# Late rounds of a fused attention and expert kernel: scores in two halves of the features, and a product in three fp32r passes instead of fp32

## The chip, the cores and the metric

One core of a Trainium2 chip. The metric is the device time of one execution in microseconds, the median over runs. Engines: PE (TensorE), DVE (VectorE), ACT (ScalarE), POOL (GpSimd) and SP, which here only issues DMAs.

## What is computed

x is (8, 1024, 256), that is N = 8192 tokens of D = 256. Attention runs over the H = 4 heads of one token, not over the sequence.

```python
xn = _layernorm(x, axis=-1)
q = (xn @ Wq + bq).reshape(b, s, h, d);  k = ...;  v = ...
c, sn = (jnp.cos(phase), jnp.sin(phase))
qr, qi = (q * c, q * sn);  kr, ki = (k * c, k * sn)
scores = (einsum('bshd,bsgd->bshg', qr, kr) + einsum('bshd,bsgd->bshg', qi, ki)) * scale
out = einsum('bshg,bsgd->bshd', softmax(scores, axis=-1), v)
s = swapaxes(out, 1, 2).reshape(b, s, h * d) @ Wo + bo
g = silu(ffn(xn))          # 8 experts, Sinkhorn gates, the best 2 of each token
x = x + s * g
```

## The kernel before

**Stages.** A preparation (layer norm, router, weights split into high and low fp32r parts) is followed by four *early rounds* of attention (q = 0 to 3), the *expert stage* (NM = 135 tiles of up to 128 tokens), and twelve *late rounds* (q = 4 to 15, QE = 4, NQ = 16). A round handles 512 tokens. The change touches the late rounds and adds some work to the expert stage.

**A round** has 24 pieces c on PE, each a 128x512 block of PSUM. Pieces 0 to 15 are q and k (x = c // 8, feature block i = c % 8): six fp32r matmuls each (high by high, high by low, low by high, for two halves of the depth, L1080). ACT writes the cosine part (L817) and DVE, after it, the sine part (L1596) of each piece into QT: a piece is *drained* when both are done. Pieces 16 to 23 are U = xn M, where M is Wv times Wo by heads (L1091): plain fp32 matmuls, two per piece, of XTJ (xn transposed and regrouped by POOL, `xtj`, L577) and M_s. ACT copies each to UN (L824), SP writes it to u_d and reads it back, regrouped, to US. The *scores* (L1027) follow the 24 pieces: four groups n, each 32 fp32 matmuls of 64x64, in two banks in turn.

**Softmax and mix.** DVE reads scores n (`soft_a`: L1484, L1488, L1489, L1490), ACT takes the exponential (L838), DVE normalizes (`soft_b`: L1495 to L1497). In the round after, DVE builds the attention operand (`spread`, L1502 to L1511) and adds the bias to US (`biased`, L1522), PE multiplies (`mix`, L1048) and DVE takes the result out (`mixed`, L1533). Here a `spread` with its `biased` is called a *pair*. Pairs stand at pieces 16, 18, 20 and 22, mixes at 18, 20, 22 and 23, PE's transposes of the next round's tokens (`xt`, L980) at 17 and 20.

**Banks.** Rotated pieces go round five PSUM banks (0, 1, 2, 6, 7), U pieces round three (0, 1, 2). `ring` makes PE wait until the piece that had the bank before is drained.

**The end of a round's tokens.** POOL adds up the two expert outputs and xn of the tokens of round q-1 (`total`, L661 to L668) while PE is in round q, ACT takes their SiLU (`silu`, L804), and POOL finishes them (`result`, L676 and L677). ACT stands in order: `silu(q - 1)` comes behind the copy of piece 18, and ACT then waits for POOL. The first four rounds' tokens are finished by the way in the *host* rounds 5, 7, 9 and 11 (a second `total`, a SiLU between the exponentials, L800), and DVE does their part (`early`, L1544 and L1545) at piece 8 of the round after. For the last round POOL does `total(14)` and `total(15)` in a row, and `silu(15)` stands at piece 23.

**Order.** All of it is written out: each engine runs its own loop over q and c and waits on counters. `s_ch` counts PE's pieces, `s_ca` ACT's, `s_cd` DVE's rotated pieces, `s_xtj` POOL's regroupings, `s_ct` its totals. WR and WM are two views of one stretch of memory of 24576 columns: expert weights in WR, then QT in columns 0 to 16383 and M_s in 16384 to 24575 of WM.

Of the kernel before, what the change touches and what calls it, by code (L numbers as in the profile page):

```python
# [5 lines left out]
F32 = mybir.dt.float32  # L6
# [15 lines left out]
QE = 4  # L22
# [14 lines left out]
def program(nc, x, phase, Wq, bq, Wk, bk, Wv, bv, Wo, bo, rw, rb, temp, wg, wp, wo, out):  # L37
# [8 lines left out]
    with ctx:  # L46
# [7 lines left out]
        m_d = nc.dram_tensor("m_d", [128, 8192], F32).ap()  # L54
        w_d = nc.dram_tensor("w_d", [E * 128, 6144], F32).ap()
# [21 lines left out]
        QT = WM[:, 0:16384].rearrange("p (x c n) -> p x c n", x=4, c=2)  # L77

        def rotated(x, i):

            v = QT[:, x, i % 2, :]
            return v.rearrange("p (t h) -> p t h", h=H)[:, :, i // 2] if x < 2 else v[:, 512 * (i // 2):512 * (i // 2) + 512]
# [3 lines left out]
        XL = sb("XL", [128, 2, 512], F32R)  # L86
        XTJ = sb("XTJ", [128, 2, 4, 128])
        UN = sb("UN", [128, 3, 512])
# [6 lines left out]
        AB = sb("AB", [128, 2, 512])  # L95
        AT = sb("AT", [128, 2, 128])
# [79 lines left out]
        def bank(g):  # L176
            q, c = divmod(g, 24)
            if c < 16:
                return ((0, 1, 2, 4, 5) if q <= QE else (0, 1, 2, 6, 7))[c % 5]
            return (c - 15) % 3  # L180

        held, prior = {}, {}
        for g in range(24 * NQ):
            prior[g] = held.get(bank(g))
            held[bank(g)] = g

        def pM(n):
# [44 lines left out]
            sem(n) for n in ("s_sa2", "s_pm", "s_u63", "s_c15", "s_z", "s_rl"))  # L232

# [56 lines left out]
        def cs(q):  # L290
            if q < NQ - 1:
                return cY1, cY2, cN, cX
            return cE1, cE2, cE3, AB[:, :, :].rearrange("p a (i d) -> p (a i) d", d=D)
# [34 lines left out]
        def _(e):  # L328
# [89 lines left out]
            def load_c(q):  # L418
# [34 lines left out]
            def segment(q0, q1):  # L453
                for q in range(q0, q1):
# [11 lines left out]
                    for c in range(8):  # L466
# [55 lines left out]
            for x in range(1, E):  # L522
# [23 lines left out]
        def _(e):  # L546
# [21 lines left out]
            def xtj(q):  # L568
# [6 lines left out]
                for k in range(2):  # L575
                    for j in range(2):
# [3 lines left out]
                            XL[:, k, :].bitcast(F32).rearrange("p (r j) -> p j r", j=4)[:, 2 * j:2 * j + 2, :], ALU.add)  # L580
                    ins.then_inc(s_xtj, 1)
# [1103 lines left out]
```

## Time and profile before

| | |
|---|---|
| median of 3 runs | 1588.54 us (1585.54 to 1590.78) |
| the profiled execution, its own time | 1590.1 us |
| its span | 1588.3 us |
| PE busy | 1530.9 us (96%) |
| DVE, ACT, POOL busy | 972.8 (61%), 728.8 (46%), 793.0 us (50%) |
| granted TensorE clock, mean | 0.988 |
| share of PE in the chain that ended last | 89% |
| PE L1091 (U), 512 records | 237.1 us |
| PE L1027 (scores), 4096 records | 129.9 us |

Busy time of an engine is the sum over its instructions, and a busy PE can still be a PE that would have had less to do. The chain of work is followed backwards from the last instruction to what released it each time. An fp32 matmul is two records in this profile, an fp32r matmul is one.

### The profile page before, as it was taken

What the parts mean: (1) busy time and instruction counts of PE and PEld (TensorE: products, weight loads), DVE (VectorE), ACT (ScalarE), POOL (GpSimd) and SP (SyncE); (2) the same over time, 40 slices, a digit from 0 to 9 for tenths busy, and PEclk for the clock granted to TensorE, in tenths of its full rate; (3) what the DMA queues carried; (4) which work ended last, traced back from release to release, by engine and by line L of the source; (5) the groups of instructions that cost most, each with busy time, mean ns of one, the idle gap of its engine ahead of it and who ended that gap; (6) DMA issues with size and microseconds to landing.
All of it is one profiled execution on the core that took longest, in us unless ns stands there. A gap on an engine that the chain in (4) does not pass through costs nothing.

```text
span 1588.3 us, 32794 instructions
## 1 busy us (share of the span) xinstructions
PE 1530.9 (96%) x11408; PEld 1166.3 (73%) x11408; DVE 972.8 (61%) x1880; ACT 728.8 (46%) x1205; POOL 793.0 (50%) x945
## 2 busy tenths in 40 slices
PE   5999699989999999999999999999999999999997
PEld 2546566668888888888888888776666776666773
DVE  7567989953333333333333333577889788888777
ACT  4766334413333333333333333546456565555552
POOL 4637589813433444433444333253574564853456
PEclk9999899989999999999999999999999999999999
DMA  9989852265233231323211231255555666455464
GB/s 327 396 314 324 301 187 78 76 217 189 68 124 108 82 126 64 97 95 111 77 54 57 71 146 51 90 167 166 172 187 189 205 200 207 156 168 172 155 206 147
DMA packets 175351, 251.23 MB, mean 158 GB/s; under 512 B 15336, under 2 KB 122656, under 8 KB 175072
## 3 DMA queue, kind: packets, MB, share of 16 engines
q1 hardware_dynamic: 160576, 211.48, 39.1%
q0 software_dynamic: 12960, 35.41, 6.8%
q8 instruction: 104, 1.70, 0.4%
q10 hardware_dynamic: 1664, 2.26, 0.4%
q14 instruction: 47, 0.39, 0.1%
HBM read 149.58 MB, written 99.50 MB: 157 GB/s over the span
## 4 chain that ended last, share of the span: by engine, by line
PE 89%; DVE 6%; DMA 2%; ACT 1%; issue 1%; SPq 1%; ACTq 0%; DVEq 0%
PE ps L1145 23%; PE ps L1080 21%; PE ps L1091 13%; PE ps L1164 12%; PE ps L1027 6%; PE ps L1154 4%; PE ps L1048 2%; PE ps L1127 2%; PE ps L996 2%; PE ps L924 1%; DMA WR<-w_d 1%; PE ps L980 1%; PE ps L914 1%; DVE UN L1230 1%; SPq L502 1%
## 5 line engine op out<-in xcount | busy, mean ns | idle before, releaser
L1145 PE MATMUL ps<-WR,FR 128*128 x1620 | 407.9, 401 | 1.9 <-DMA WR<-w_d 1.8
L1145 PEld LDWEIGHTS ps<-WR,FR 128*128 128x128 f32 x1620 | 296.2, 189 | 60.2 <-issue 3.0
L649 POOL DMA_INDIRECT y_d<-AUX x135 | 133.3, 987 | 351.6 <-ACT AUX L868 351.6
L1656 DVE TENSOR_TENSOR AUX<-AUX,ps 128x512 f32<-128x512 f32 x135 | 92.9, 688 | 342.0 <-ACT AUX L856 342.0
L817 ACT ACTIVATE WM<-ps,bcs,trig 128x512 f32<-128x512 f32 x256 | 252.2, 1016 | 85.9 <-PE ps L1080 78.9
L1596 DVE TENSOR_SCALAR WM<-ps,vec,trig 128x512 f32<-128x512 f32 x256 | 243.6, 993 | 61.2 <-ACT WM L817 60.5
L1091 PE MATMUL ps<-WM,XTJ 128*128 128x512 f32 x512 | 237.1, 600 | 0.0
L856 ACT ACTIVATE AUX<-ps 128x512 f32<-128x512 f32 x135 | 80.9, 599 | 318.5 <-PE ps L1145 318.5
L1080 PE MATMUL ps<-XH,WH 128*128 128x512 f32 x512 | 204.8, 400 | 6.1 <-issue 3.8
L1164 PE MATMUL ps<-WR,ABR 128*128 x1080 | 209.4, 292 | 0.0
L1080 PE MATMUL ps<-XH,WL 128*128 128x512 f32 x512 | 199.7, 390 | 0.0
L1080 PE MATMUL ps<-XL,WH 128*128 128x512 f32 x512 | 199.6, 390 | 0.0
L645 POOL DMA_INDIRECT AUX<-xn_d,AUX x135 | 131.7, 975 | 77.2 <-issue 40.1
L1164 PEld LDWEIGHTS ps<-WR,ABR 128*128 128x128 f32 x1080 | 165.5, 190 | 0.0
L1091 PEld LDWEIGHTS ps<-WM,XTJ 128*128 128x128 f32 x512 | 91.7, 190 | 96.5 <-issue 93.8
L661 POOL TENSOR_TENSOR AUX<-AUX,GP 128x256 f32<-128x256 f32 x128 | 80.3, 662 | 148.3 <-DMA AUX<-in_L_attn_x_dram 144.5
L1164 PE MATMUL ps<-WR,FR 128*128 x540 | 152.1, 282 | 0.0
L1027 PE MATMUL ps<-WM 128*64 128x64 f32 x4096 | 129.9, 227 | 16.8 <-DVE TM L1484 16.0
L1027 PEld LDWEIGHTS ps<-WM 128*64 128x64 f32 x4096 | 126.2, 142 | 25.5 <-DVE TM L1484 16.7
L824 ACT ACTIVATE UN<-ps 128x512 f32<-128x512 f32 x128 | 76.2, 595 | 139.0 <-PE ps L1091 135.9
L1080 PEld LDWEIGHTS ps<-XH,WH 128*128 128x128 f32 x512 | 96.3, 188 | 27.3 <-issue 5.2
L1080 PEld LDWEIGHTS ps<-XH,WL 128*128 128x128 f32 x512 | 96.1, 188 | 20.4
(238 smaller groups left out, 2199.1 us busy)
## 6 DMA issues: line engine op xcount, KB each, us to landing
US<-u_d SPq DMA_DIRECT2D x63, 512.0 KB, 5.4
u_d<-UN SPq DMA_DIRECT2D x120, 256.0 KB, 2.0
WR<-w_d SPq DMA_DIRECT2D x96, 256.0 KB, 6.0
AUX<-y_d SPq DMA_DIRECT2D x32, 512.0 KB, 5.6
WM<-in_L_attn_x_dram SPq DMA_DIRECT2D x16, 512.0 KB, 9.5
xn_d<-WM SPq DMA_DIRECT2D x32, 256.0 KB, 7.3
w_d<-USR SPq DMA_DIRECT2D x16, 512.0 KB, 4.9
AUX<-xn_d SPq DMA_DIRECT2D x16, 512.0 KB, 6.1
```

What stands on the lines that cost most here:

```text
L645: e.indirect_dma_start(XG[:, m % 2, :], None, xn_d, bass.IndirectOffsetOnAxis(gidx[:, m:m + 1], 0)).then_inc(s_g[m % 2], 16)
L649: e.indirect_dma_start(y_d, bass.IndirectOffsetOnAxis(toks[:, m - 5:m - 4], 0), YS[:, (m - 5) % 2, :], None).then_inc(s_y[(m - 5) % 2], 16)
L661: ins = e.tensor_tensor(y[:, i, :], y[:, i, :], GP[:, i, k, q, None].broadcast_to([128, D]), ALU.mult)
L817: e.activation(rotated(2 * x, i), b, ACT.Identity, bias=bcs[:, x, 0, i:i + 1], scale=trig[:, 0, i:i + 1]).then_inc(s_ca, 1)
L856: e.activation(GR[:, :], mG[m % 2][:, :], ACT.Relu).then_inc(s_gr, 1)
L1027: mm = e.matmul(pS[n % 2][row:row + 64, 64 * c:64 * c + 64].rearrange("p (g t) -> p g t", g=H), QT[:, x, h, col:col + 64], QT[:, 2 + x, h, ...
L1080: mm = e.matmul(b[:, :], w[:, k, 128 * c:128 * c + 128], xx[:, k, :], start=(k == 0 and w is WH and xx is XH), stop=(k == 1 and w is WL))
L1091: mm = e.matmul(b[:, :], XTJ[:, k, a // 2, :], M_s[:, k, 512 * a:512 * a + 512], start=(k == 0), stop=(k == 1))
L1145: mm = e.matmul(b[:, :], x, WR[:, bass.ds(off[m] + (2048 * z + 1024 * a + 512 * k), 512)], start=(k == 0 and x is xh and z == 0), stop=(k ...
L1164: mm = e.matmul(mY[m % 2][:, 0:256], x, WR[:, bass.ds(off[m] + (4096 + 1024 * z + 256 * c), 256)], start=(c == 0 and x is hh and z == 0), ...
L1596: e.tensor_scalar(rotated(2 * x + 1, i), ps[bank(24 * q + c)][:, :], bqk[:, x, i:i + 1], trig[:, 1, i:i + 1], ALU.add, ALU.mult).then_inc( ...
L1656: e.tensor_tensor(HS[:, m % 2, :], GR[:, :], mP[m % 2][:, :], ALU.mult).then_inc(s_h, 1)
```

## The change

It applies to the late rounds only.

1. **U in three fp32r passes.** M is kept as a high and a low part (MH, ML). Each U piece is six fp32r matmuls (XHJ by MH, XHJ by ML, XLJ by MH, for two depths) instead of two fp32 ones. POOL's `xtj` (four additions) becomes `xj` (eight copies, of the high and of the low part of xn).
2. **The split of M** is made in the expert stage: sixteen times, once in every seven tiles, ACT issues the load of a 128x512 piece of m_d to UN, DVE splits it (`split_m`, one copy and one subtraction), and ACT issues the store to mhl_d. SP then loads ML and MH (2 x 2 MB and 4 x 1 MB) at the expert stage's end, where it loaded M_s (4 x 1 MB).
3. **Room.** ML takes columns 0 to 8191, MH 16384 to 24575, so that the rotated q and k have 8192 to 16383 (QH), half of what QT had.
4. **Order.** Since QH holds either the even or the odd feature blocks, a late round now runs: the eight even rotated pieces (P0), U 16 to 19, the first half of the scores (`half_scores(q, 0)`, all four groups), the eight odd rotated pieces (P1), U 20 to 23, the second half of the scores. The last round runs P0, U 16 to 23, first half, P1, second half, then its four mixes. Mixes stand at 18, 19, 21, 23, pairs at 16, 17, 19, 20, transposes at 20 and 22; in the last round mixes and pairs keep their places. `soft_a(n)` starts when the second half of the scores of both groups of a bank is there.
5. **Banks.** P0 takes banks 0, 1, 6, 7, 2, 0, 1, 2 in this order (0, 1, 4, 5, 2, 0, 1, 2 in round 4), U 16 to 19 takes 0, 1, 2, 0, P1 takes 1, 2, 6, 7, 0, 1, 2, 0, and U 20 to 23 takes 1, 2, 0, 1.
6. **The x of the last tokens** is loaded late (`load_x`), to the columns of ML that pieces 16 and 17 of the last round have used.

`silu(q - 1)` is still written at piece 18, `early` at piece 8 and `silu(15)` at piece 23; nothing in `total`, `result`, `store_c` or `load_c` of rounds before the last is changed.

```diff
+        def order(q):
+            if q < QE:
+                return tuple(range(24))
+            if q < NQ - 1:
+                return P0 + (16, 17, 18, 19) + P1 + (20, 21, 22, 23)
+            return P0 + tuple(range(16, 24)) + P1
...
+        BANKS = {c: (0, 1, 6, 7, 2, 0, 1, 2)[i] for i, c in enumerate(P0)}
+        BANKS.update({c: (1, 2, 6, 7, 0, 1, 2, 0)[i] for i, c in enumerate(P1)})
...
+            def xj(q):
+                e.wait_ge(s_xtd, 2 * q + 2)
+                e.wait_ge(s_ch, 24 * q)
+                if q == QE:
+                    e.wait_ge(s_dn, NM)
+                for k in range(2):
+                    for v, w in ((XHJ, XH), (XLJ, XL)):
+                        for j in range(2):
+                            ins = e.tensor_copy(v[:, k, 2 * j:2 * j + 2, :],
+                                                w[:, k, :].rearrange("p (r j) -> p j r", j=4)[:, 2 * j:2 * j + 2, :])
                     ins.then_inc(s_xtj, 1)
...
+            def half_scores(q, h):
+                e.wait_ge(s_ca, at(q, 14 + h))
+                e.wait_ge(s_cd, rotated_by[q, 14 + h])
+                if h == 0:
+                    e.wait_ge(s_sm1, 4 * q)
+                for i in range(4):
+                    for c in range(4):
+                        for x in range(2):
+                            for a in range(2):
...
+                                mm = e.matmul(pS[i // 2][row:row + 64, to:to + 64].rearrange("p (g t) -> p g t", g=H),
+                                              QH[:, x, col:col + 64],
...
+                    if h == 1:
+                        mm.then_inc(s_s, 1)
...
                             for k in range(2):
-                                mm = e.matmul(b[:, :], XTJ[:, k, a // 2, :], M_s[:, k, 512 * a:512 * a + 512],
-                                              start=(k == 0), stop=(k == 1))
...
+                                for xx, w in ((XHJ, MH), (XHJ, ML), (XLJ, MH)):
+                                    mm = e.matmul(b[:, :], xx[:, k, j, :], w[:, k, cols],
+                                                  start=(k == 0 and xx is XHJ and w is MH), stop=(k == 1 and xx is XLJ))
...
+                        if q >= QE and c == (23 if q == NQ - 1 else 19):
+                            half_scores(q, 0)
+                    if q >= QE:
+                        half_scores(q, 1)
+                        continue
```

ACT in a late round after round 5, where `silu` stands. Before, it comes behind sixteen rotated pieces and three U pieces:

```order
L817 ACTIVATE WM<-ps7,bcs,trig 128x512
L817 ACTIVATE WM<-ps0,bcs,trig 128x512
L824 ACTIVATE UN<-ps1 128x512
L824 ACTIVATE UN<-ps2 128x512
L753 ACTIVATE XH<-ps3 128x512
L824 ACTIVATE UN<-ps0 128x512
L804 ACT_TABLE_LOAD
L804 ACTIVATE AUX<-AUX 128x1024
L824 ACTIVATE UN<-ps1 128x512
```

The same place in the changed kernel; the rows L903 above the fence are the last of P0, those below `silu` (L890) the first of P1:

```order
L903 ACTIVATE WM<-ps1,bcs,trig 128x512
L903 ACTIVATE WM<-ps2,bcs,trig 128x512
L912 ACTIVATE UN<-ps0 128x512
L912 ACTIVATE UN<-ps1 128x512
L912 ACTIVATE UN<-ps2 128x512
L890 ACT_TABLE_LOAD
L890 ACTIVATE AUX<-AUX 128x1024
L912 ACTIVATE UN<-ps0 128x512
L903 ACTIVATE WM<-ps1,bcs,trig 128x512
L903 ACTIVATE WM<-ps2,bcs,trig 128x512
```

Eight rotated pieces and three U pieces now stand ahead of `silu` in a round, where sixteen and three did; eight rotated pieces stand behind it, where none did.

DVE at the end of the rotated pieces of a late round before (L1596 the last rotation, L1502 to L1522 a pair, L1464 the low part of the next round's tokens, L1533 `mixed`):

```order
L1596 TENSOR_SCALAR WM<-ps0,vec,trig 128x512
L1502 TENSOR_TENSOR AC<-SA,mask8 128x128
L1506 STREAM_TRANSPOSE AC<-AC 128x128
L1507 TENSOR_REDUCE AH<-AC 128x16
L1511 TENSOR_TENSOR AT<-AH,maskr 128x128
L1522 TENSOR_TENSOR US<-US,BR 128x1024
L1464 TENSOR_TENSOR XL<-ps3,XH 128x512
```

and in the changed kernel behind P0:

```order
L1741 TENSOR_SCALAR WM<-ps2,vec,trig 128x512
L1647 TENSOR_TENSOR AC<-SA,mask8 128x128
L1651 STREAM_TRANSPOSE AC<-AC 128x128
L1652 TENSOR_REDUCE AH<-AC 128x16
L1656 TENSOR_TENSOR AT<-AH,maskr 128x128
L1667 TENSOR_TENSOR US<-US,BR 128x1024
L1647 TENSOR_TENSOR AC<-SA,mask8 128x128
```

The second pair follows the first at once, and both stand behind the eighth rotated piece instead of the sixteenth.

## Rows read from the trace of the kernel before

**Rows 1.** Chain of work, late rounds: start us, length us, what (x records)

```profile
1092.70 7.62 PE ps L1027 x256
...
1139.74 7.62 PE ps L1027 x256
...
1453.99 3.43 PE ps L1091 x8
...
1459.58 0.57 PE ps L1048 x8
...
1464.35 0.59 PE ps L980 x4
...
1471.42 7.62 PE ps L1027 x256
1479.04 21.98 PE ps L1080 x96
...
1518.46 7.62 PE ps L1027 x256
...
1564.82 3.91 PE ps L1027 x128
```

**Rows 2.** Timeline of DVE, softmax behind the scores of round 13

```profile
1474.61 1.19 DVE L1490 TENSOR_TENSOR SS<-SS,sx 128x16 f32<-128x16 f32 x1
...
1481.28 0.17 DVE L1490 TENSOR_TENSOR SS<-SS,sx 128x16 f32<-128x16 f32 x1
...
1482.89 4.32 DVE L1596 TENSOR_SCALAR WM<-ps,vec,trig 128x512 f32<-128x512 f32 x4 [0.43 <-ACT WM L817]
```

**Rows 3.** Timeline of POOL: regrouping, then first and last piece of `total(13)`

```profile
1473.49 4.53 POOL L577 TENSOR_TENSOR XTJ<-XH,XL 128x256 f32<-128x256 f32 x4
1490.11 4.62 POOL L661 TENSOR_TENSOR AUX<-AUX,GP 128x256 f32<-128x256 f32 x8 [12.09 <-DMA AUX<-in_L_attn_x_dram]
...
1497.71 2.83 POOL L668 TENSOR_TENSOR AUX<-AUX 128x256 f32<-128x256 f32 x4
```

**Rows 4.** Timeline of POOL, last pieces of `total(5)`, `total(6)` and `total(15)`

```profile
1124.92 3.93 POOL L668 TENSOR_TENSOR AUX<-AUX 128x256 f32<-128x256 f32 x4
...
1168.25 2.79 POOL L668 TENSOR_TENSOR AUX<-AUX 128x256 f32<-128x256 f32 x4
...
1558.15 3.86 POOL L668 TENSOR_TENSOR AUX<-AUX 128x256 f32<-128x256 f32 x4
```

**Rows 5.** Timeline of DVE: a last rotation, pairs alone, pairs beside POOL

```profile
1454.84 0.81 DVE L1596 TENSOR_SCALAR WM<-ps,vec,trig 128x512 f32<-128x512 f32 x1 [0.55 <-ACT WM L817]
...
1459.18 0.28 DVE L1502 TENSOR_TENSOR AC<-SA,mask 128x128 f32<-128x128 f32 x1
...
1461.62 0.42 DVE L1533 TENSOR_TENSOR AUX<-ps,bo_b 128x256 f32<-128x256 f32 x1
...
1468.78 1.23 DVE L1522 TENSOR_TENSOR US<-US,BR 128x1024 f32<-128x1024 f32 x1 [0.74 <-DMA US<-u_d]
...
1552.97 0.70 DVE L1502 TENSOR_TENSOR AC<-SA,mask 128x128 f32<-128x128 f32 x1
...
1556.68 0.41 DVE L1533 TENSOR_TENSOR AUX<-ps,bo_b 128x256 f32<-128x256 f32 x1
```

**Rows 6.** Timeline of DVE, second half of `early` in round 6

```profile
1115.74 1.23 DVE L1545 TENSOR_TENSOR AUX<-AUX 128x1024 f32<-128x1024 f32 x1
```

**Rows 7.** Timeline of ACT: `silu(12)`, then rotations behind the exponentials

```profile
1461.53 1.06 ACT L804 ACTIVATE AUX<-AUX 128x1024 f32<-128x1024 f32 x1
...
1481.61 10.71 ACT L817 ACTIVATE WM<-ps,bcs,trig 128x512 f32<-128x512 f32 x9
```

**Rows 8.** Timeline of the SP queue: the read-back issued after piece 19

```profile
1463.57 1.04 SPq L399 DMA_DIRECT2D US<-u_d  x1
```

**Rows 9.** One line each: duration ns min/median/max; L1490 from 200 to 560 us

```profile
L616 POOL CAST USR<-US x16: 609/612/1163, 117.1 to 180.7; 128x512 fp32r<-128x512 f32 x16
...
L1490 DVE TENSOR_TENSOR SS<-SS,sx x12: 174/176/368, 226.1 to 342.0; 128x16 f32<-128x16 f32 x12
```

More of the change, by code:

```diff
@@ L298, in us, with piece @@
             return XB[:, :, :] if n == 4 * NQ - 1 else US[:, n % 3, :, :]
+        def piece(i):
+            return slice(512 * i, 512 * i + 512)
+        raw_at, split_at, kept_at = ({7 * i + d: i for i in range(16)} for d in (2, 4, 6))
         def blk(ap, q):
@@ L428, in load_c, with load_x @@
                     e.dma_start(xx[h:128:4], rows(xf, q)[h]).then_inc(sl, 16)
+            def load_x():
+                e.wait_ge(s_ch, at(NQ - 1, 17))
+                for h in range(H):
+                    e.dma_start(cs(NQ - 1)[3][h:128:4], rows(xf, NQ - 1)[h]).then_inc(s_xe, 16)
             def load_e(k):
@@ L811, in segment @@
                 for q in range(q0, q1):
-                    for c in range(24):
-                        e.wait_ge(s_ch, 24 * q + c + 1)
-                        b = ps[bank(24 * q + c)][:, :]
+                    for c in order(q):
+                        e.wait_ge(s_ch, at(q, c))
+                        b = ps[bank(q, c)][:, :]
                         if c < 16:
                             x, i = c // 8, c % 8
-                            e.activation(rotated(2 * x, i), b,
+                            e.activation(rotated(q, 2 * x, i), b,
                                          ACT.Identity, bias=bcs[:, x, 0, i:i + 1],
@@ L1074, in segment @@
                     e.wait_ge(s_xtd, 2 * q + 2)
-                    for c in range(24):
-                        b = ring(24 * q + c)
+                    for c in order(q):
+                        b = ring(q, c)
                         if c < 16:
@@ L1107, in segment @@
                         scores(4 * q + i)
-                        if q == NQ - 1 and i >= 2:
-                            mix(4 * q + i - 2)
                         place(lists.get((q, 24 + i), ()))
                 if q1 == NQ:
-                    mix(4 * NQ - 2)
-                    mix(4 * NQ - 1)
+                    e.wait_ge(s_ca, at(NQ - 1, 15))
+                    e.wait_ge(s_cd, rotated_by[NQ - 1, 15])
+                    for i in range(4):
+                        mix(4 * NQ - 4 + i)
             e.wait_ge(s_wsp, 4)
@@ L1591, in segment @@
                 for q in range(q0, q1):
[L1592 removed]
+                    for c in order(q):
                         if c < 16:
[L1594 removed]
+                            e.wait_ge(s_ca, at(q, c))
                             x, i = c // 8, c % 8
[L1596 to L1597 removed]
+                            e.tensor_scalar(rotated(q, 2 * x + 1, i),
+                                            ps[bank(q, c)][:, :], bqk[:, x, i:i + 1], trig[:, 1, i:i + 1],
                                             ALU.add, ALU.mult).then_inc(s_cd, 1)
```

178 lines of the change are left out of this document (129 added, 49 removed).

## The prediction, made before the changed kernel ran

> **What bounds the kernel now.** First the page and the chain of work: PE is busy 96% of the span and is 89% of the chain. The chain of the late rounds, in order of time, then shows what a round is: a repeating block of PE pieces with no other engine in it. I count from S, the start of the scores. S is at 1471.42 and next at 1518.46, so round 14 takes 47.04 us; from S the scores take 7.62 us and then the next round's rotations begin [rows 1]. Then the timelines of DVE, ACT and POOL around S, to see how far behind PE they are: in before nothing they do late reaches PE, and the question is what a shorter and reordered PE does to that.
>
> **Part 1, what PE saves.** Eight records of U take 3.43 us, 0.429 each, and a round has 32: 13.7 us. 96 fp32r matmuls take 21.98 us, 0.229 each [rows 1]; the 48 that replace the 32 records stream the same 512 columns from operands of the same kind, so 11.0 us. The saving is 2.74 us a round, 33 us in twelve rounds. A U piece now takes 1.37 us, as a rotated piece does. ACT empties it in the 0.6 us it took before, which PE's piece hides. The scores keep their 64x64 matmuls: two halves of 3.81. PE's own work is 47.04 - 2.74 = 44.3 us a round. If nothing waited the sum would end here, at 1590.1 - 33 = 1557.
>
> **Part 2, the cover of the softmax shrinks.** Before, 7.62 us of scores lie between S and the next rotation; now only the second half, 3.81. The softmax starts no earlier: its first group was complete 1.9 us after S (a quarter of 7.62), and now two of the four groups are complete half way through 3.81, again 1.9. DVE does it and ACT's exponentials in sequence, then the rotations. DVE's first rotation behind it starts at 1482.89 and is one of four in 4.32 us, so it is done at 1483.97 = S + 12.55 [rows 2]. Call this D. Two of DVE's operations in it took 1.19 us or more where the same one takes 0.17 otherwise [rows 2], both while POOL's regrouping ran (4.53 us for four additions [rows 3]). The eight new copies are not in the trace. Nearest are POOL's casts of 128x512, 0.61 us each [rows 9], and the additions, 1.13; eight are between 2.4 us (half the columns at half of 0.61) and 9.1. I take 5, by the casts, since they have one input too. Each can hold DVE for less: beside POOL's one-input marks the same operation took 0.37 us at most [rows 9]. So D is between S + 10.5 (both holds gone) and 12.55; I take 11.3. The Trainium skill says the same in kind (SBUF — State Buffer, Who interferes with whom): a DVE instruction with two SBUF inputs contends with a GpSimd instruction that reads SBUF, and the later one fully blocks. By that rule alone, copies whose sum is longer than the additions' would give D = 12.55, and with it some 15 us more than my sum.
>
> PE starts P0 at S + 3.81 with five free banks and reaches piece 10 at 10.7; piece 10 needs piece 0 drained, D. Worse is piece 14: it shares bank 2 with piece 8, the fifth, drained at D + 4 x 1.08 (the pace of [rows 2]) = D + 4.3, where PE would come by at 3.81 + 7 x 1.37 = 13.4. P0 thus ends at D + 5.7 = 17.0, not at 14.8: **2.2 us of wait** (1.4 to 3.4 for the two ends of D).
>
> **Part 3, the pairs.** The last rotation was drained 1.66 us after PE's piece (1455.65 against 1453.99 [rows 1, 5]). A pair with `mixed` takes from 1459.18 to 1461.62, 2.44 us; beside POOL's `total` 3.7 [rows 5]. Behind P0 DVE has two pairs in a row, PE three U pieces, a mix (0.57 [rows 1]), a fourth piece and a mix. From the end of P0: first pair ready at 1.7 + 2.5 = 4.2, PE there at 4.1; second at 6.7, PE at 6.2. That is 0.6 us of wait. `total` ran from 1490.11, S + 18.7 [rows 3], right where these pairs now stand (S + 18.7 to 24); beside it both pairs at 3.5 make 2.4 us. I take **1.5 us**. The transposes and mixes behind P1 find DVE idle before.
>
> A plain round is then 44.3 + 2.2 + 1.5 = **48.0 us, 0.9 more than before**.
>
> **Part 4, `silu` stands in front of P1.** `total(q-1)` starts on data whose loads SP issues behind the stores of the round before; nothing of that chain is changed, it hangs on S. It ended at 1497.71 + 2.83, S + 29.1, in round 14 [rows 3]; at S + 36.2 in round 6 (1124.92 + 3.93 against 1092.70) and S + 31.3 in round 7 (1168.25 + 2.79 against 1139.74) [rows 1, 4]. ACT reached `silu` in time before, having drained all sixteen rotations. Now it stands there with the copy of piece 19 and all of P1 queued behind it. PE meanwhile does piece 19, the first half of the scores and four rotations; its fifth, piece 9, needs bank 0 from piece 19. After the total: SiLU 1.06 us [rows 7], the copy 0.6, five rotations at 1.15 (nine took 10.71 [rows 7]), and DVE's 1.08: piece 9 is drained 8.4 us after the total's end, and only then may piece 15 have its bank. P1 ends at 8.4 + 1.4 = 9.8 after it. Behind P1 stand four U pieces (5.5), two transposes of at most 0.59 and two mixes: 7.8 us. So a round cannot be shorter than **the total's end + 17.6**: 46.7 in rounds 13 and 14 (not the limit), 48.9 in round 7 (and 9, 11), 53.8 in round 6 (and 8, 10, 12, each behind a host round). That is +1.9 for three rounds and +6.7 for four. In these four `early` (two operations like the one of 1.23 us [rows 6]) also stands in the middle of P0 on DVE; by itself it would make them about 50.5, so it is hidden under the larger limit.
>
> **Part 5, the first and the last round.** Round 4 saves 2.74, now includes the first half of the scores before S (+3.81), and waits 1.5 at the mixes: +2.6. Round 15 took 46.4 (1518.46 to 1564.82 [rows 1]). `silu(14)` ends at about S + 31, and only then can piece 19 be copied and written and the read-back of the mix's fourth group be issued; one took 5.2 us from its issue to DVE's use [rows 5, 8], so the fourth mix is done at about 39 and the first half of the scores at 43. `silu(15)` needs `total(15)`, which ended at S + 43.6 [rows 1, 4]. P1's eleven us and the drain of its last piece, 1.7, now uncovered, give about 55.6: +9. Behind the last S the same DVE sequence starts 1.9 us later as before: 0.
>
> **Part 6, hidden.** In the expert stage ACT gets 32 DMA issues, DVE 16 times some 1.3 us (a copy and a subtraction of 128x512), DMA 12 MB more. PE is never out of work there and the other engines are idle for more than half of each tile; the loads that moved end tens of microseconds before round 4, as the old ones did. 0, at worst 5 us.
>
> **Sum.** +2.6 (round 4), 3 x 0.9 = 2.7 (5, 13, 14), 3 x 1.9 = 5.7 (7, 9, 11), 4 x 6.7 = 26.8 (6, 8, 10, 12), +9 (15): 46.8 us. Part 3's and part 4's limits leave some slack to each other, and a later PE gives POOL more room; I take 44. The profiled execution took 1590.1, of which 1588.3 is span; 1634 for it, and 1.6 us less against the median: **1632 us**.
>
> **Rivals.** (a) *Nothing waits*: faster. It needs D below S + 9.1 (so that piece 14 finds its bank at 13.4) and the total's end below S + 26.7. Then each round is 44.3 and the time about 1557. For it: PE had no wait in any late round. Against: D without any hold is 10.5, and no total ended before 29.1. (b) *The order costs, `silu` does not*: the totals end earlier than in before, or ACT's queue is caught up; then the four rounds behind a host round are 50.5 (+3.5), three at +0.9, round 15 about +5: 2.6 + 5.4 + 14 + 5 = 27, about 1614. (c) *Contention is full*: D at 12.55, pairs at 3.5, totals stretched by another 1.5 us; plain rounds 50.1, the eleven rounds limited by totals 1.5 longer: about 70 more, 1658. (d) *The waits and the saving cancel*: D = 10.5 and 0.6 at the mixes make plain rounds 46.3; with `early` alone in four rounds the sum is near zero, 1589. That U does not reach 1.37 us a piece is unlikely; even 1.45 costs 0.6 a round and is in the range.
>
> **How the numbers follow.** Forecast 0.55; (b) 0.18, (c) 0.12, (a) 0.09, (d) 0.06. The range reaches from the lower part of (b), 1604, to the lower part of (c), 1655. Faster by over 0.3% (about what a measurement of this kernel can tell from no change): 0.10; within: 0.04; slower: 0.86.
>
> **What would show it.** Right: U records of 0.229 us; a wait of PE at its sixth and eighth rotated piece for DVE; waits at two mixes for `biased`; ACT idle for POOL at `silu` by 5 to 12 us and PE waiting for ACT or DVE late in P1; rounds 6, 8, 10, 12 longer than 5, 13, 14 by some 5 us. Wrong if the round lengths are alike (part 4 fails), if D is under S + 10 (part 2), or if all rounds are near 44.3.

## The result, and the profile after

The changed kernel took **1646.38 us** (median of 4 runs, 1643.18 to 1650.45) against 1589.66 us for the kernel before beside it: a ratio of 1.034 (95% interval 1.032 to 1.037). It is slower by 57 us; 1632 was predicted, in a range of 1604 to 1655. The profiled execution took 1650.45 us.

The page of the changed kernel: its busy line, and the line of the chain that ended last, by engine.

```profile
span 1648.7 us, 33347 instructions
...
PE 1525.0 (92%) x11600; PEld 1203.3 (73%) x11600; DVE 965.1 (59%) x1912; ACT 717.2 (43%) x1205; POOL 812.7 (49%) x993
...
PE 63%; DVE 12%; DMA 7%; POOL 6%; SPq 6%; ACT 3%; issue 3%; ACTq 0%; DVEq 0%
```

PE was 89% of that chain before and is 63% now. DVE, POOL and the DMAs have come into it. What PE waits for from the first late round on (reason, us in total, times, longest):

```profile
PE ps L1208 <- DVE WM L1741: 29.0, 37, 2.3
PE ps L1176 <- issue: 11.2, 11, 2.9
PE ps L1176 <- DVE US L1667: 6.0, 8, 1.2
PE ps L1227 <- ACT WM L903: 5.8, 4, 1.5
PE ps L1208 <- ACT UN L912: 5.1, 6, 1.4
```

L1208 are the rotated pieces, L1227 is U, L1176 the mixes. The "issue" of a mix is mostly the second pair on DVE, as the rows of round 14 below show. In the kernel before, the same stretch had 8.6 us of waits in all, nearly all behind the last scores.

I cut the two profiled executions at the same places: the first product of the expert stage, the first late rotation, and S, the start of each round's scores (in the changed kernel, of their second half).

| | before | after | difference | predicted |
|---|---|---|---|---|
| up to the expert stage | 347.2 | 349.9 | +2.7 | 0 |
| expert stage | 659.0 | 665.3 | +6.3 | 0, at worst 5 |
| round 4, up to S | 39.4 | 41.4 | +2.0 | +2.6 |
| round 5 | 47.0 | 52.7 | +5.7 | +0.9 |
| rounds 6, 8, 10, 12 | 47.0 to 47.1 | 52.0 to 52.8 | +21.5 | +26.8 |
| rounds 7, 9, 11 | 47.2 to 48.3 | 50.1 to 50.7 | +7.8 | +5.7 |
| rounds 13, 14 | 47.0 | 49.9, 50.1 | +6.0 | +1.8 |
| round 15 | 46.4 | 57.0 | +10.6 | +9 |
| behind the last S | 23.6 | 21.5 | -2.1 | 0 |

**One round behind a host round.** PE in round 10, its rows with a wait, from S to the next S. They answer rows 1, where no such row stands.

```profile
1315.10 3.95 PE L1153 MATMUL ps<-WM 128*64 128x64 f32 x128
1327.59 0.47 PE L1208 MATMUL ps<-XH,WH 128*128 128x512 f32 x1 [1.51 <-DVE WM L1741]
1331.29 0.47 PE L1208 MATMUL ps<-XH,WH 128*128 128x512 f32 x1 [0.70 <-DVE WM L1741]
1334.36 0.70 PE L1227 MATMUL ps<-WR,XHJ 128*128 128x512 f32 x2 [1.44 <-ACT WM L903]
...
1341.17 0.64 PE L1176 MATMUL ps<-US,AT 128*32 128x256 f32 x8 [0.29 <-issue]
1341.74 4.02 PE L1153 MATMUL ps<-WM 128*64 128x64 f32 x128
1352.37 0.50 PE L1208 MATMUL ps<-XH,WH 128*128 128x512 f32 x1 [0.94 <-ACT UN L912]
1354.84 0.47 PE L1208 MATMUL ps<-XH,WH 128*128 128x512 f32 x1 [0.82 <-DVE WM L1741]
1358.54 0.47 PE L1208 MATMUL ps<-XH,WH 128*128 128x512 f32 x1 [0.70 <-DVE WM L1741]
...
1367.86 1.33 PE L1153 MATMUL ps<-WM 128*64 128x64 f32 x38
```

(The last row is cut off where the view ended.) The chain of work of the same stretch says where the three waits of L1208 behind 1341.74, those in P1, come from:

```profile
1347.92 2.83 POOL AUX L753 x4
1350.75 0.02 issue
...
1351.73 0.58 ACT UN L912
1352.31 1.17 ACT WM L903
...
1353.50 4.90 DVE WM L1741 x5
...
1358.54 1.62 PE ps L1208 x6
1360.16 1.39 PE ps L1227 x6
```

POOL's `total` ends at 1350.75 (L753), `silu` runs, then ACT copies piece 19, rotates, DVE drains five pieces, and only then may PE do the last of P1. ACT had waited 10.10 us for POOL (answer to rows 7):

```profile
1350.77 1.06 ACT L890 ACTIVATE AUX<-AUX 128x1024 f32<-128x1024 f32 x1 [10.10 <-POOL AUX L753]
1351.73 0.58 ACT L912 ACTIVATE UN<-ps 128x512 f32<-128x512 f32 x1
```

The next S is 17.1 us after the total's end. This holds in every round from 6 to 13 (17.07 to 17.14), not only behind host rounds; in round 14 it is 18.9.

**A plain round.** DVE, POOL and PE in round 14 (S = 1520.17), around the two pairs:

```profile
1539.01 0.66 DVE L1647 TENSOR_TENSOR AC<-SA,mask 128x128 f32<-128x128 f32 x1
...
1540.78 1.63 DVE L1667 TENSOR_TENSOR US<-US,BR 128x1024 f32<-128x1024 f32 x1
1542.34 0.69 DVE L1647 TENSOR_TENSOR AC<-SA,mask 128x128 f32<-128x128 f32 x1
...
1544.39 1.75 DVE L1667 TENSOR_TENSOR US<-US,BR 128x1024 f32<-128x1024 f32 x1
```

```profile
1537.75 5.75 POOL L746 TENSOR_TENSOR AUX<-AUX,GP 128x256 f32<-128x256 f32 x8 [10.74 <-DMA AUX<-in_L_attn_x_dram]
1543.58 3.84 POOL L750 TENSOR_TENSOR AUX<-AUX 128x256 f32<-128x256 f32 x4
1547.50 3.83 POOL L753 TENSOR_TENSOR AUX<-AUX 128x256 f32<-128x256 f32 x4
```

```profile
1542.67 0.64 PE L1176 MATMUL ps<-US,AT 128*32 128x256 f32 x8 [1.16 <-DVE US L1667]
...
1546.24 0.64 PE L1176 MATMUL ps<-US,AT 128*32 128x256 f32 x8 [1.34 <-issue]
```

The pairs take 3.3 and 3.7 us beside the sums (2.4 alone), and the sums take 13.6 us beside the pairs (10.4 in rows 3): they stretch each other. Record by record, the three of POOL's sixteen operations that lie beside a `biased` (L1667) took 1.59 to 1.71 us, the others 0.61 to 0.79. The second mix starts when the second pair ends.

**Expert stage.** SP issued the two loads of ML, 2 MB each, at 897.86; the gather of one tile came late, and the product behind the gap took 4.60 instead of 3.00 us:

```profile
910.22 0.44 PE L1269 MATMUL ps<-ident,AUX 128*128 128x128 f32 x2 [0.99 <-DMA AUX<-xn_d,AUX]
911.48 4.60 PE L1287 MATMUL ps<-WR,FR 128*128 x12 [0.82 <-issue]
```

```profile
911.60:915.80 4.20, 4.20 (x12) 3.30 (x13) 0.00 (x0) 0.00 (x0) 0.59 (x1) 0.59 0.17 55
```

Stops of this size do not always do that: in run 4 PE stood for 1.09 and 0.66 us at the same place, and the product took 3.02.

**The last round.** The longest wait of a late round stands there, 4.58 us at a U piece: ACT waits for `total(14)` at `silu(14)`, with the copies of the U pieces behind it.

```profile
1603.03 1.22 PE L1227 MATMUL ps<-WR,XHJ 128*128 128x512 f32 x2 [4.58 <-ACT UN L912]
```

### The profile page after: what moved, and what is told of

Same layout as the page of the kernel before. It is cut to its first block, busy times and chain, and to the rows that moved or that the text cites. A ratio compares the mean times of both kernels' runs of the same rounds, so it can differ in the third digit from the quotient of the medians.

```text
span 1648.7 us, 33347 instructions
## 1 busy us (share of the span) xinstructions
PE 1525.0 (92%) x11600; PEld 1203.3 (73%) x11600; DVE 965.1 (59%) x1912; ACT 717.2 (43%) x1205; POOL 812.7 (49%) x993
## 4 chain that ended last, share of the span: by engine, by line
PE 63%; DVE 12%; DMA 7%; POOL 6%; SPq 6%; ACT 3%; issue 3%; ACTq 0%; DVEq 0%
PE ps L1287 21%; PE ps L1306 11%; PE ps L1208 10%; PE ps L1227 4%; DVE WM L1741 4%; PE ps L1296 3%; POOL AUX L746 3%; DMA AUX<-in_L_attn_x_dram 2%; PE ps L1153 2%; PE ps L1223 2%; DMA WR<-w_d 2%; POOL AUX L750 2%; PE ps L1103 2%; PE ps L1269 2%; SPq L568 2%
## 5 line engine op out<-in xcount | busy, mean ns | idle before, releaser
L734 POOL DMA_INDIRECT y_d<-AUX x135 | 138.9, 1029 | 351.8 <-ACT AUX L956 351.8
L1741 DVE TENSOR_SCALAR WM<-ps,vec,trig 128x512 f32<-128x512 f32 x256 | 234.1, 992 | 121.9 <-ACT WM L903 121.4
L903 ACT ACTIVATE WM<-ps,bcs,trig 128x512 f32<-128x512 f32 x256 | 238.5, 1013 | 91.4 <-PE ps L1208 86.5
L1208 PE MATMUL ps<-XH,WH 128*128 128x512 f32 x512 | 210.8, 412 | 39.8 <-DVE WM L1741 29.9
L1208 PE MATMUL ps<-XL,WH 128*128 128x512 f32 x512 | 200.7, 392 | 0.0
L1208 PE MATMUL ps<-XH,WL 128*128 128x512 f32 x512 | 200.5, 392 | 0.0
L746 POOL TENSOR_TENSOR AUX<-AUX,GP 128x256 f32<-128x256 f32 x128 | 88.3, 724 | 139.6 <-DMA AUX<-in_L_attn_x_dram 136.7
L1208 PEld LDWEIGHTS ps<-XH,WH 128*128 128x128 f32 x512 | 96.6, 189 | 77.4 <-ACT WM L903 45.3
L1227 PE MATMUL ps<-WR,XHJ 128*128 128x512 f32 x384 | 125.6, 409 | 10.4 <-ACT WM L903 5.8
L1208 PEld LDWEIGHTS ps<-XH,WL 128*128 128x128 f32 x512 | 96.5, 188 | 21.4
L1208 PEld LDWEIGHTS ps<-XL,WH 128*128 128x128 f32 x512 | 96.8, 189 | 16.9 <-issue 0.2
L676 POOL TENSOR_SCALAR OH<-AUX 128x128 bf16<-128x128 f32 x96 | 95.0, 1001 | 24.3 <-DVE AUX L1573 15.6
L1784 DVE TENSOR_TENSOR FR<-ps,FR 128x256 fp32r<-128x256 f32 x135 | 57.2, 424 | 84.1 <-ACT FR L937 81.3
```

The lines of the kernel that those rows point to most:

```text
L676: e.tensor_scalar(rank1h[:, j % 16, :], ior_f, slot_p[:, k, n:n + 1], mark[:, k, n:n + 1], ALU.is_equal, ALU.mult).then_inc(s_oa, 1)
L734: e.indirect_dma_start(y_d, bass.IndirectOffsetOnAxis(toks[:, m - 5:m - 4], 0), YS[:, (m - 5) % 2, :], None).then_inc(s_y[(m - 5) % 2], 16)
L746: ins = e.tensor_tensor(y[:, i, :], y[:, i, :], GP[:, i, k, q, None].broadcast_to([128, D]), ALU.mult)
L903: e.activation(rotated(q, 2 * x, i), b, ACT.Identity, bias=bcs[:, x, 0, i:i + 1], scale=trig[:, 0, i:i + 1]).then_inc(s_ca, 1)
L1208: mm = e.matmul(b[:, :], w[:, k, 128 * c:128 * c + 128], xx[:, k, :], start=(k == 0 and w is WH and xx is XH), stop=(k == 1 and w is WL))
L1227: mm = e.matmul(b[:, :], xx[:, k, j, :], w[:, k, cols], start=(k == 0 and xx is XHJ and w is MH), stop=(k == 1 and xx is XLJ))
```

## The experiments

Each is an edit of the changed kernel. All of them in one table, lengths of rounds in us from the profile of each:

| kernel | median us | round 5 | 6, 8, 10, 12 | 7, 9, 11 | 13, 14 | 15 |
|---|---|---|---|---|---|---|
| changed kernel | 1646.4 | 52.7 | 52.0-52.8 | 50.1-50.7 | 49.9, 50.1 | 57.0 |
| 1 SiLU behind P1 | 1623.4 | 56.3 | 48.9-50.5 | 47.7-48.6 | 47.7, 49.1 | 51.6 |
| 2 U in fp32 | 1659.6 | 55.0 | 53.6-54.3 | 51.0-51.6 | 51.6, 50.7 | 58.3 |
| 3 copies behind the softmax | 1638.6 | 49.8 | 51.7-52.0 | 49.8-50.4 | 49.8, 48.6 | 58.8 |
| 4 sums early | 1636.1 | 55.7 | 50.1-51.4 | 48.6-49.1 | 48.7, 48.7 | 54.1 |
| 5 ML last | 1641.2 | 49.2 | 52.5-52.8 | 49.5-50.9 | 50.2, 49.3 | 58.3 |
| 6 mixes behind the half scores | 1647.4 | 53.4 | 52.1-53.2 | 49.9-50.9 | 50.4, 47.0 | 58.7 |
| 7 moves 1, 3, 5, 6, banks, `early` | 1580.8 | 44.9 | 45.4-46.3 | 45.1-46.4 | 44.9, 44.9 | 51.4 |
| 8 = 7 and 4 | 1589.6 | 44.8 | 45.6-46.3 | 48.1-49.6 | 44.8, 44.8 | 52.6 |
| 9 = 7 with U in fp32 | 1599.6 | 47.1 | 47.7 | 47.3-47.4 | 47.4, 47.1 | 49.2 |
| 10 = 7, x loaded behind | 1576.4 | 44.9 | 45.4-45.5 | 45.2-46.2 | 44.9, 44.8 | 49.2 |
| 11 = 7 without 6 | 1595.5 | 49.8 | 46.3-47.6 | 46.4-47.4 | 45.7, 48.4 | 51.1 |

The kernel before had medians of 1589.7 us beside the changed kernel, 1593.6 beside runs 1 to 4 and 1592.0 beside runs 5 to 11, so between rows of different groups a difference of less than some 4 us says little. Row 5 is a single execution. Round 5 has a source of scatter of its own, which run 1 shows.

**1. The SiLU behind P1.**

```diff
-                        if q > QE and c == 18:
+                        if q > QE and c == (23 if q == NQ - 1 else 20):
                             silu(q - 1)
-                        if q == NQ - 1 and c == 23:
+                        if q == NQ - 1 and c == P1[3]:
                             silu(q)
```

> The SiLU of the previous round's tokens now stands behind all of P1 (behind the copy of piece 20), where POOL's sums have long ended; in the last round it stands at piece 23 and silu(15) in the middle of P1. Theory: only the rounds behind a host round (6, 8, 10, 12, measured 52.0 to 52.8 us) were set by the sums' end; they fall to the length of the others, about 50.1, and the waits of 0.4 to 1.4 us for ACT in P1 of rounds 7, 9 and 11 go too (0.7 us each). The last round loses its wait of 4.6 us for ACT at a U piece, of which some comes back behind the last scores. Together 4 x 2.4 + 3 x 0.5 + 3 = 14 us less than the changed kernel, about 1632. Rival, the place of the SiLU is not what makes these rounds long (the early operations on DVE or the order itself do): the same within 3 us, 1646.

Measured 1623.41 us, 23 us less than the changed kernel. The gain is in all rounds from 6 on, 1.5 to 3.8 us in rounds 6 to 13, whose length a total's end had set, and 5.4 in the last: my own expectation had still taken rounds 7, 9, 11, 13 and 14 as limited elsewhere. Rounds 6, 8, 10 and 12 are still longer than rounds 7, 9, 11 and 13; they alone have `early` in P0 and a wait of 1.4 us at the first U piece, but no run moves `early` alone. Round 5 got 3.6 us longer, by something that stands ahead of its SiLU, in code that the edit does not touch. Here is why, DVE and POOL of that kernel behind S = 1053.28:

```profile
1056.60 5.79 DVE L1635 TENSOR_TENSOR SS<-SS,sx 128x16 f32<-128x16 f32 x1
```

```profile
1056.52 1.25 POOL L664 CAST ABR<-XL 128x256 fp32r<-128x256 f32 x2
1057.71 4.65 POOL L746 TENSOR_TENSOR AUX<-AUX,GP 128x256 f32<-128x256 f32 x8
```

A subtraction of 128x16 that takes 0.17 us alone stood 5.79 us, until POOL's run of copies and multiplications had its first pause at 1062.36. PE then waited 6.56 us at the sixth rotated piece, and 2.35 us in the changed kernel, where the same subtraction took 1.18. The profiles of runs 4 and 6 have the long hold too, some 4 us of their round 5 that their edits did not make.

**2. U in two fp32 matmuls, in the new order.**

```diff
+                                mm = e.matmul(b[:, :], XHJ[:, k, j, :].bitcast(F32), MH[:, k, cols].bitcast(F32),
+                                              start=(k == 0), stop=(k == 1))
+                                continue
                                 for xx, w in ((XHJ, MH), (XHJ, ML), (XLJ, MH)):
```

> The changed order with U as two plain fp32 matmuls of the high parts, as long as before the change; the low parts of M and of the tokens are left out of U here, so the output is less exact. What differs from the changed kernel is the 2.74 us a round that the three passes were meant to save. Theory: part of the saving is swallowed by waits. A longer U covers the wait of PE for the pairs (2.5 us a plain round) and the sums of POOL, so only the four pieces behind P1, and one or two ahead of it, show: 1.4 to 2 us a round, 12 x 1.7 = 20, about 1666. Rival, the saving reaches the end whole and the loss is the order's alone: 12 x 2.74 = 33, 1679. Second rival, nothing of it reaches the end: 1646.

Measured 1659.60, 13 us more: less than half of the 33 that the three passes save on paper reaches the end in this order.

**3. The copies behind the softmax.**

```diff
                 if q == QE:
                     e.wait_ge(s_dn, NM)
+                else:
+                    e.wait_ge(s_sub, 4 * q)
```

> POOL's eight copies of the tokens' parts wait until DVE has done the last subtraction of the softmax, in rounds after the first late one; nothing else moves. Theory: the copies hold DVE's subtractions (0.67 to 1.18 us where the same operation takes 0.17), so the first rotation behind the softmax comes 1.0 us earlier in most rounds and 2.4 us earlier in round 5, and PE's wait at its sixth rotated piece (1.0 us, in round 5 2.4) goes. Rounds 7, 9, 11, 13 and 14: -0.9 each; round 5: -2.3; rounds 6, 8, 10, 12, set by the sums: 0; last round: 0 to -0.9. About 7 us less, 1639. Rival, the holds cost nothing because ACT's rotation sets the pace: the same, 1646. Rival, the copies now run beside the rotations and the first U piece waits for them: slower.

Measured 1638.63, 7.8 us less, as expected in sum but not in its parts (see below). DVE's subtractions are back at 0.18 us, here behind the scores of round 13:

```profile
1513.16 0.18 DVE L1637 TENSOR_TENSOR SS<-SS,sx 128x16 f32<-128x16 f32 x1
```

The wait at the sixth rotated piece is gone in that round; the one at the eighth, for the drain of the fifth, whose bank it takes, is still there:

```profile
1524.40 0.47 PE L1210 MATMUL ps<-XH,WH 128*128 128x512 f32 x1 [0.67 <-DVE WM L1743]
```

Round 5 got 2.9 us shorter, rounds 6 to 13 by 0.2 to 1.0, round 14 by 1.5, and the last one 1.8 longer. Expected were 0.9 in each of rounds 7, 9, 11, 13 and 14 and nothing in 6, 8, 10 and 12: that the sum came out is in part luck.

**4. The sums start early.** The sum waits for its own three loads (a semaphore of their own), and these are issued ahead of the stores.

```diff
                 e.wait_ge(s_ro, 4 * (q - QE) + 4)
+                if q + 1 < NQ - 1:
+                    load_y(q + 1)
...
-                    e.wait_ge(*((s_cl, 112 * (q - QE + 1)) if q < NQ - 1 else (s_c15, 48)))
+                    e.wait_ge(*((s_cl, 48 * (q - QE + 1)) if q < NQ - 1 else (s_c15, 48)))
```

> POOL's sum of the last round's tokens no longer waits for the load of x, which it does not read, and its own three loads are issued ahead of the stores of the results. Theory: it starts 5 to 7 us earlier, at about S + 11 instead of S + 17.6 (S is the start of the second half of the scores). The rounds behind a host round fall from 52.4 to about 50. The sum no longer runs beside DVE's two pairs, so PE's waits at the two mixes (1.2 and 1.3 us) shrink to 0.6 together, as in round 4: -2 for rounds 7, 9, 11, 13, 14. Altogether 4 x 2.4 + 9 x 1.5 = 23 us less, 1623. Rival, the start of the sums is set elsewhere (POOL's own queue): the same within 3 us.

Measured 1636.11: 10 us less, not 23 (round 5, with the long hold, is 3.0 us longer in its profile). In round 10 the sum starts at S + 19.9 instead of 22.9 and ends at S + 33.5 instead of 35.6, since all of it now lies beside the pairs. The waits at the mixes did not go (0.78 and 1.46 us in round 14): the sums moved, but not away from the pairs. The expectation had the sum start at about S + 11; the loads landed later, and in rounds 6 to 14 it started at S + 15.6 to 20.6.

**5. ML last.**

```diff
-            for k in range(2):
-                if k == 1:
-                    spent(5)
-                e.dma_start(ML[:, k, :].bitcast(F32), mhl_d[:, 1, 4096 * k:4096 * k + 4096]).then_inc(s_mlo[k], 16)
             spent(6)
...
+            e.wait_ge(s_ml[3], 16)
+            for k in range(2):
+                e.dma_start(ML[:, k, :].bitcast(F32), mhl_d[:, 1, 4096 * k:4096 * k + 4096]).then_inc(s_mlo[k], 16)
+                e.wait_ge(s_mlo[k], 16)
```

> The low part of M is loaded behind the high part, one 2 MB piece after the other, instead of ahead of it in one go; nothing else moves. Theory: in the changed kernel these two loads make the gather of one tile's tokens late (PE idle 0.6 to 1.8 us, in two of five profiles with a first product of 4.6 instead of 3.0 us behind it). The wait at that tile goes, no other comes in its place before round 4, and the expert stage is 1.3 to 3.9 us shorter than the 661 to 665 us of the profiles so far. Rival, whatever 8 MB are loaded there collides with the gathers: a wait of the same size stands 20 to 40 us later.

One execution, 1641.15 us; its round 5 is 3.5 us shorter than in the profile of the changed kernel, which the place of ML did not make. The wait at about 910 us is gone and none stands later, but the stage took 663.9 us, since this happened elsewhere:

```profile
514.61 0.44 PE L1269 MATMUL ps<-ident,AUX 128*128 128x128 f32 x2 [1.20 <-DMA AUX<-xn_d,AUX]
516.35 4.59 PE L1287 MATMUL ps<-WR,FR 128*128 x12 [1.30 <-DMA WR<-w_d]
```

At the place of the wait, all six profiles with ML early have a gather late by 0.32 to 1.09 us, and none of the six with ML last: that wait comes with the two loads. Over all profiles the stage takes 660.8 to 665.3 us with ML early (six, mean 663.0), 660.2 to 663.9 with ML last (six, mean 661.7), and 659.0 before. The means put 1.3 us to the place of ML, less than the spread of one kind, so what it is worth over the whole stage is not settled. The rest stands as waits for weights and tokens among the added loads and stores of M; no run here takes these away alone.

**6. The mixes behind the first half of the scores**, in rounds 4 to 14.

```diff
-                            mix(4 * q - 4 + mixes(q)[c])
+                            if not (QE <= q < NQ - 1 and c in (18, 19)):
+                                mix(4 * q - 4 + mixes(q)[c])
...
                             half_scores(q, 0)
+                            if c == 19:
+                                mix(4 * q - 4)
+                                mix(4 * q - 3)
```

> In rounds 4 to 14 PE does the first half of the scores ahead of the two mixes that stood at pieces 18 and 19, instead of behind them. Theory: the two pairs on DVE, stretched by POOL's sums beside them, are what PE waits for there (1.2 and 1.3 us, and about 0.15 more each to fill up again); the 4 us of scores cover them. Rounds 5, 7, 9, 11, 13 and 14 lose up to 2.8 us, but P1 is then nearer to the SiLU, which allows no less than the sums' end + 17, 48.2: -1.9 each. Rounds 6, 8, 10 and 12, already at that limit: 0. About -11, 1635. Rival, DVE is the bound of the round and the wait only moves to P1 (its third pair now stands ahead of P1's first rotation): the same, 1646.

Measured 1647.41: nothing in sum (round 14 alone got 3.1 us shorter). The mixes wait no more, and PE waits as long in P1 for piece 19's copy behind the SiLU, here in round 10:

```profile
1347.14 0.50 PE L1208 MATMUL ps<-XH,WH 128*128 128x512 f32 x1 [1.68 <-ACT UN L912]
1349.61 0.47 PE L1208 MATMUL ps<-XH,WH 128*128 128x512 f32 x1 [0.81 <-DVE WM L1745]
1353.31 0.47 PE L1208 MATMUL ps<-XH,WH 128*128 128x512 f32 x1 [0.71 <-DVE WM L1745]
```

Rounds 6 to 14 end 17.1 us after the total. My expectation of 48.2 had put the plain totals' ends at S + 31.2, round 14's in the changed kernel; in rounds 7, 9, 11 and 13 they are at S + 32.8 to 33.8.

**7 and 8. The moves together.** Runs 1, 3, 5 and 6 in one, with `early` at piece 21 and other banks:

```diff
-        BANKS = {c: (0, 1, 6, 7, 2, 0, 1, 2)[i] for i, c in enumerate(P0)}
-        BANKS.update({c: (1, 2, 6, 7, 0, 1, 2, 0)[i] for i, c in enumerate(P1)})
+        BANKS = {c: (0, 1, 6, 7, 2, 0, 1, 6)[i] for i, c in enumerate(P0)}
+        BANKS.update({c: (0, 1, 6, 7, 2, 0, 1, 2)[i] for i, c in enumerate(P1)})
...
-                        if q - 1 in host and c == 8:
+                        if q - 1 in host and c == 21:
```

> Five moves together: the SiLU behind P1, the eight copies behind the softmax, the mixes behind the first half of the scores, early at piece 21, the low part of M loaded last; and P0's last piece in bank 6 (bank 4 in round 4) instead of 2, with the banks behind it moved on, so that it no longer waits for the fifth piece's drain. Theory: the waits at the sixth and eighth rotated piece, at the mixes and in P1 are then all but gone, and a round is PE's own 44.6 plus 0.5 to 1 of drain and first-rotation waits: 10 rounds of 45.4, the last one about 50, 21.5 behind it, 1050 ahead of it. About 1576, faster than the kernel before by 1%. Rival, POOL and DVE block each other elsewhere for as much (copies beside rotations, sums beside pairs): 48 a round, 1602.

> The same with POOL's sums started early (they do not wait for x, and their loads are issued ahead of the stores). Theory: with the SiLU moved nobody waits for the sums in time, so nothing is gained from their end; they now run beside DVE's rotations rather than beside the pairs, which PE no longer waits for either: within 3 us of the kernel without this move. Rival, the pairs stretched by the sums still set P1's first drains: 5 to 10 us less.

Version 7 took 1580.82 us, 0.993 of the kernel before (0.990 to 0.995). Rounds 5, 13 and 14 are 44.9 us, where the prediction had 44.3 for PE alone; in 5 and 14 PE has no wait of 0.3 us or more. The shares of `early` and of the banks were not taken apart: no run has either alone. Version 8 took 1589.63, 9 us more, which neither expectation had: rounds 7, 9 and 11 grew by 2.2 to 3.2 us. ACT and PE in its round 11:

```profile
1360.28 0.60 ACT L926 ACTIVATE UN<-ps 128x512 f32<-128x512 f32 x1 [13.00 <-DMA u_d<-UN]
```

```profile
1360.93 0.50 PE L1222 MATMUL ps<-XH,WH 128*128 128x512 f32 x1 [2.37 <-ACT UN L926]
```

SP issues in order. Its load of x waits until the stores of the results have landed; behind the earlier loads that wait ended at 1346.20 = S + 18.9 (in version 7 at S + 13.3), the writes of U started at S + 26.2 (S + 19.8), and ACT had no free buffer for piece 19. In version 7 the same copy waits 9.71 us, just short of costing anything.

**9. Version 7 with U in fp32.**

> The version with all moves but the early loads (1580.8), with U as two plain fp32 matmuls of the high parts as before the change; the low parts are left out of U, so the output is less exact. Theory: where PE waits for nothing, the three passes are worth what the rows say, 2.74 us a round in twelve rounds: +33 at most, less 0.5 us a round where ACT's wait for the write of U is now covered: +27 to +33, 1608 to 1614. Rival, in this order too part of U lies beside other engines' work, as in the changed kernel, where the same edit cost 13 us: +13, 1594.

Measured 1599.63, 19 us more, between the two. Rounds 5 and 14, in which version 7 has no wait to cover, grow by 2.2 us and not by 2.74: that is what the three passes are worth where PE waits for nothing. Rounds 7, 10 and 11 grow by 0.9 to 1.4, since a U of the old length covers part of what version 7 still waits for; the last round gets 2.2 us shorter, and its wait of 2.76 us at a mix is gone.

**10. x loaded behind the read-back**, on version 7.

```diff
                                 load_u(4 * q - 1)
+                                if q > QE + 1:
+                                    load_xx(q - 1)
...
+            def load_xx(q):
+                if QE < q:
+                    e.wait_ge(s_o, 64 * (q - QE))
+                for h in range(H):
+                    e.dma_start(cs(q)[3][h:128:4], rows(xf, q)[h]).then_inc(s_cx, 16)
```

> The version with all moves but the early loads, and SP issues the load of the last tokens' x behind the read-back that follows piece 19, instead of ahead of that round's writes of U; the sum waits for its own three loads alone. Theory: the writes of U no longer stand behind a wait for stores, so ACT's copy of piece 19 does not wait 10 us for a free buffer; rounds 7, 10 and 11 (46.0 to 46.4) and the last (51.4) get shorter by 1 us and by 1 to 2: 3 to 6 us less, 1576. The sums start about 4 us earlier and run beside DVE's last rotations. Rival, as in the version with the early loads they then stretch something PE waits for: 3 to 9 us more.

Measured **1576.42 us**, 0.990 of the kernel before (0.988 to 0.992), faster than both. Of the rounds named, 10, 11 and the last got shorter, by 0.9, 1.3 and 2.2 us; round 7 did not. Its page:

```profile
PE 1503.5 (96%) x11600; PEld 1202.9 (76%) x11600; DVE 964.1 (61%) x1912; ACT 727.9 (46%) x1205; POOL 813.8 (52%) x993
...
PE 77%; DVE 8%; ACT 4%; DMA 4%; SPq 3%; issue 2%; POOL 2%; ACTq 0%; DVEq 0%; POOLq 0%
```

**11. Version 7 without the move of the mixes.**

> The version with all moves but the early loads, with the mixes back in front of the first half of the scores. That move alone was worth nothing in the changed kernel, where every round from 6 to 13 ended 17.1 us after the sums' end. Theory: with the SiLU out of the way the two mix waits (1.2 and 1.3 us, and 0.3 to fill up) come back whole: rounds 5 to 14 at 2.5 more, 1580.8 + 10 x 2.5 = 1606. Rival, the move is worth nothing here either, since the wait then stands elsewhere: 1581.

Measured 1595.47: the move that was worth nothing alone is worth 15 us here, not the 25 expected. Rounds 5 and 14 got 4.9 and 3.5 us longer, the others up to 1.9.

## Why the prediction held, and where it was off

Part 1 was right about a piece: six records of U take 1.39 us in the chain above (1.37 predicted). A whole round is 44.9 us where PE waits for nothing (version 7), not 44.3, so that 2.2 us are saved and not 2.74: in round 14 of version 7 the 48 records of U with their change-overs to other work take 12.0 us (14.3 before, where the prediction had 11.0 for 13.7), and the two halves of the scores 7.76 for 7.62. That nobody sees the saving whole was right too.

Part 2 was right in cause and size: the eight copies take 4.7 us (5 taken); in round 14 the first rotation is done at S + 11.7 (11.3) and PE waits 0.98 and 0.70 us, and some 0.15 more each to start again, 2.0 in all (2.2). Run 3 shows the copies as the cause of the first of these waits; the second is for the bank that the eighth piece shares with the fifth. What I did not see is round 5, where a sum follows the copies at once: its first rotation is done at S + 13.1, or S + 17.3 where the long hold falls into it. PE's waits of 0.3 us or more in that round add up to 7.3 us, and it was 5.7 us longer than before where I had 0.9.

Part 3 was too small. Of "both pairs at 3.5 make 2.4 us" I took 1.5; the pairs took 3.3 and 3.7 and PE waited 1.16 and 1.34, 2.8 with the restarts.

Part 4 had the mechanism and the constant (17.6; measured 17.1; nine rotations in 10.71 us are 1.19 each, not the 1.15 it used) and missed a term of it: **the ends of the totals**. I took them from before, S + 29.1 and 31.3 in plain rounds. But part 3 had just put the pairs beside the totals, and a hold costs both sides: the sum of round 14 takes 13.6 instead of 10.4 us, and ends are at S + 31.2 to 33.6. So the limit reached all of rounds 6 to 13, and plain rounds were 50 where I had 48.0 and 48.9: 1.2 to 1.8 us too little in rounds 7, 9 and 11, and 2 in round 13. Behind host rounds the ends (34.9 to 35.6) were near the old ones, and 52.0 to 52.8 came for 53.8. Runs 1 and 6 show that it is this limit, and run 6 that the mix waits of part 3 do not add to it. That the pairs made the sums longer rests on the records that lie beside each other: no run moves the pairs away from them.

Part 5: round 4 by 2.0 (2.6), the last round by 10.6 (9), behind the last S -2.1 (0).

Part 6 was the other miss: +6.3 in the profiled execution, +3.3 in the mean of the twelve profiles, where I had 0. "PE is never out of work" holds only as long as the gathers and weights arrive. One gather is late because of ML's two loads (run 5); why weights are late in other places stays open. The 2.7 us ahead of the expert stage are no part of the change as far as the traces show: over the twelve profiles that point lies between 344.5 and 350.8 us.

The sum: the parts gave 46.8, and I took 44, since a later PE would give POOL more room. It was the other way round, and nearly all misses have one sign: 60.4 us in the profiled execution. The rounds behind a host round, by 5.3 us together, and what stands behind the last S, by 2.1, came out shorter than predicted, and this hid part of the rest. Rounds 6, 8, 10 and 12 are 2 to 3 us longer than 13 and 14, not the 5 given as the sign, and about as long as round 5.

The rivals: (a), 44.3 a round, is what versions 7 and 10 come near to, once the waits are moved away. (b) is refuted by run 1, which gains 23 us by the SiLU's place, and (d) by the plain rounds of 50 us. (c), at 1658, was as near to the measured 1646 as the forecast of 1632: it named the plain round of 50.1 and the stretched totals.

## What to carry to other kernels

When a step is moved beside work of an engine that it holds up, as DVE's pairs and POOL's sums here, both get longer: put the longer time of each into every later limit. Two waits in one period may be limits in parallel, not in series: then removing one alone gives nothing (run 6), and its worth shows only when the others are gone (run 11). An instruction that waits in a strictly ordered queue, such as a SiLU on ACT or a load on SP that waits for stores, should stand where what it waits for has long been done.

## What the runs showed of the hardware

The hold of DVE by POOL has no fixed price. The first subtraction behind round 4, with the same code around it, took 5.8 us in three profiles (runs 1, 4 and 6), and 1.18, 1.17 and 0.62 in three others (the changed kernel, runs 2 and 5); with the copies moved away, 0.17. The 5.8 us ended at a pause of POOL's stream, not at the end of one instruction; why the hold is long in one execution and short in another stays open. The Trainium skill (SBUF — State Buffer, Who interferes with whom) says that the port pair which DVE and GpSimd share is an exclusive lock. The rows agree that one side stands, but not that it stands for one instruction of the other: here the block outlasted a run of ten.

PE's wait as this profile gives it understates what a stop costs. In round 14:

```profile
1530.75 0.39 PE L1208 MATMUL ps<-XH,WL 128*128 128x512 f32 x1
1532.12 0.47 PE L1208 MATMUL ps<-XH,WH 128*128 128x512 f32 x1 [0.98 <-DVE WM L1741]
```

Matmuls follow each other every 0.23 us but last 0.39 each. The 0.98 is counted from the end of the 0.39; from the pace of 0.23 the stop cost 1.14. If each of the five stops of that round costs 0.16 us more in this way, that is 0.8 us which the list of waits does not show (an estimate: only stops between two L1208 rows were read).
